# A fused state-space and attention block on one core: front chunks on five PSUM banks, scores of the first stretch from step 6, keys in three transfers

## What is computed

```python
x = x + _L0_conv_ref(_gn(x), ...)      # selective scan block
x = x + _L1_conv_ref(_gn(x), ...)      # attention block

# L0: 96 -> 2*192 channels, depthwise 3x3 conv, four scans of 2304 steps
xz = einsum('bchw,oc->bohw', x, in_proj_w);  xx, z = split(xz, 2)
xx = gelu(depthwise3x3(xx) + conv_b)
xs = stack([x_hw, x_wh, reversed x_hw, reversed x_wh])
dts, Bs, Cs = split(einsum('bkdl,kcd->bkcl', xs, x_proj_w), [R, R + N])
delta = softplus(einsum(dts, dt_w) + dt_b)
h = h * exp(delta * A) + (delta * u) * B;  y = sum_n(h * C)    # 16 states
y = layernorm(sum of the four directions + u * Ds) * gelu(z);  out = out_proj(y)

# L1: 96 -> 3*96 channels, depthwise 3x3 conv, 8 heads of 12
q, k = l2norm(q), l2norm(k)
out = softmax(q @ k.T * SCALE) @ v;  out = w_proj(out)
```

## Time and profile before

| | us |
|---|---|
| median of 3 runs | 11364.33 |
| lowest, highest | 11346.41, 11385.92 |
| the profiled execution's own time | 11346.75 |
| its span in the profile | 11344.6 |
| PE busy | 8357.5 (74%) |
| DVE busy | 7439.6 (66%) |
| ACT busy | 6430.6 (57%) |
| POOL busy | 6332.1 (56%) |

### The profile page before, as it was taken

One profiled execution on the slowest core, in us unless ns is written; L12 is line 12 of the kernel. 1 busy time (PEld: TensorE's weight loads), 2 busy tenths in 40 slices (PEclk: granted clock), 3 DMA queues, 4 the chain that ended last, 5 costly groups with the idle time before them and its releaser, 6 DMA issues.

```text
span 11344.6 us, 176742 instructions
## 1 busy us (share of the span) xinstructions
PE 8357.5 (74%) x54832; PEld 2687.9 (24%) x54832; DVE 7439.6 (66%) x6473; ACT 6430.6 (57%) x11876; POOL 6332.1 (56%) x4464
## 2 busy tenths in 40 slices
PE   6486568887687866888668777678768885588758
PEld 2122222222222222222222222222222221122212
DVE  0588638884488834888358773778548886788630
ACT  1243237773477724776257653667437773577558
POOL 0477527773377724777247662667427774577430
PEclk6565568886798866888678886888768896799779
DMA  1456415653256513555145550555415652455310
GB/s 44 143 181 196 143 49 173 185 175 95 89 183 181 175 52 117 177 178 161 49 150 176 173 166 24 171 184 174 129 54 172 182 178 78 144 184 179 116 23 19
DMA packets 772558, 1537.24 MB, mean 136 GB/s; under 512 B 89368, under 2 KB 416836, under 8 KB 762640
## 3 DMA queue, kind: packets, MB, share of 16 engines
q1 hardware_dynamic: 771600, 1525.54, 44.1%
HBM read 1272.74 MB, written 252.44 MB: 134 GB/s over the span
## 4 chain that ended last, share of the span: by engine, by line
PE 42%; issue 16%; ACT 13%; DVE 12%; DMA 8%; SPq 4%; POOL 4%; ACTq 1%; DVEq 0%; POOLq 0%
PE ps L1549 8%; PE ps L1615 8%; PE ps L1509 6%; ACT probs_buf L1060 4%; PE ps L1537 4%; DVE rings L1281 4%; DVE ps L1260 3%; DMA rep<-xd_scratch 3%; DVE job_buf L1281 2%; ACT rings L1051 2%; PE ps L1703 2%; PE ps L1704 2%; DMA job_u<-u_scratch 2%; PE ps L1566 2%; PE ps L1524 1%
## 5 line engine op out<-in xcount | busy, mean ns | idle before, releaser
L1060 ACT ACTIVATE probs_buf<-ps 128x384 f32<-128x384 f32 x6912 | 3137.8, 491 | 1884.1 <-PE ps L1615 1836.8
L880 POOL TENSOR_TENSOR hc_buf<-rings,rep 128x768 f32<-128x768 f32 x1152 | 2091.6, 1816 | 1711.0 <-DVE rings L1281 1693.8
L1615 PE MATMUL ps<-qp_buf,kp_buf 108*128 108x384 bf16 x6912 | 2299.7, 357 | 623.0 <-ACT probs_buf L1060 274.8
L1260 DVE TENSOR_TENSOR ps<-ps,rep 128x768 f32<-128x768 f32 x2304 | 2182.0, 947 | 826.6 <-PE ps L1525 683.6
L880 POOL TENSOR_TENSOR hc_buf<-job_buf,rep 128x768 f32<-128x768 f32 x1152 | 2092.1, 1816 | 948.7 <-DVE job_buf L1281 941.3
L1537 PE MATMUL ps<-hc_buf,sum_states 128*32 128x144 f32 x24576 | 1530.5, 338 | 135.7 <-POOL hc_buf L880 135.7
L1549 PE MATMUL ps<-probs_buf,v_buf 128*13 128x384 f32 x13824 | 1606.1, 540 | 32.4 <-ACT probs_buf L1060 18.4
L1524 PE MATMUL ps<-st_buf,pick_channel 96*128 96x512 bf16 x2304 | 1009.2, 438 | 652.5 <-DMA qp_buf<-qk_scratch 287.6
L1281 DVE TENSOR_TENSOR_SCAN job_buf<-rings,ps 128x768 f32<-128x768 f32 x768 | 1368.5, 1782 | 167.6 <-ACT rings L1051 142.2
L1615 PEld LDWEIGHTS ps<-qp_buf,kp_buf 108*128 108x128 bf16 x6912 | 652.7, 98 | 3065.6 <-ACT probs_buf L1060 1827.1
L1051 ACT ACTIVATE st_buf<-st_buf,a_cols 128x768 f32<-128x768 f32 x1152 | 1063.2, 927 | 271.4 <-DMA st_buf<-delta_scratch 271.1
(11 more groups left out here) (172 smaller groups left out, 8518.7 us busy)
## 6 DMA issues: line engine op xcount, KB each, us to landing
st_buf<-delta_scratch SPq DMA_DIRECT2D x1152, 384.0 KB
rings<-delta_scratch SPq DMA_DIRECT2D x1152, 384.0 KB
part_scratch<-job_buf SPq DMA_DIRECT2D x1152, 72.0 KB, 3.2
st_buf<-part_scratch SPq DMA_DIRECT2D x192, 432.0 KB, 7.1
rep<-xd_scratch SPq DMA_DIRECT2D x192, 384.0 KB
job_u<-u_scratch SPq DMA_DIRECT2D x192, 192.0 KB
delta_scratch<-job_buf SPq DMA_DIRECT2D x192, 192.0 KB, 4.9
qp_buf<-qk_scratch SPq DMA_DIRECT2D x864, 36.0 KB
```

The costliest lines, as they stand in the source:

```text
L880: pool.tensor_tensor(hc[tile % 2][:, chunk(kk, v)], h_ring[t % 2], rep_third(1, kk, v), ALU.mult).then_inc(s["hc_ready"], 1)
L1060: act.activation(probs[(m % 2) * HG + h], bank(slots["score", p]), ACT.Exp, scale=SCALE)\
L1260: dve.tensor_tensor(u_slot(t), u_slot(t), rep_third(0, kk, t % SPT), ALU.mult)\
L1615: pe.matmul(bank(slots["score", p]), k_parts[:, h, m * 128:(m + 1) * 128], q_ring[:, (kk * NS + q) % 2, h, :], start=True, stop=True).then ...
```

## The change

1. **Front chunks between the scans** (`start` and `back`, not those inside the scan of batch 0). The two projections go to banks 0 and 1, the two convolutions to banks 2 and 3, x_proj to bank 6. The copy of the first convolution is gone: gelu reads both from PSUM. PE issues the projection of chunk c+1 between the convolutions and the x_proj of chunk c, and ACT fills the pads of chunk c+1 right after the gelus of chunk c. SP loads chunk c+1 of the input before it waits for the gelus of chunk c. Since banks 0 to 3 are used, PE waits for chunk 2's pads before the layer norm, and for all copies of q, k, v before the convolutions of chunk 2.
2. **`FRONT_UNITS`, `FRONT_SUMS`**: ACT takes up the gelu part after products 3, 6, 9, 12 and the x_proj copy after products 4, 7, 10, 13; POOL transposes after sums 4, 7, 10, 13.
3. **First stretch of a batch's attention, beside a scan** (`LATE = 6`): no pieces in steps 0 to 5, four to a step in steps 6 to 23. The wait for the queries moves from the head of the stretch to piece 0. The queries of stretch 1 are loaded at steps 12 to 14 instead of 1 to 3.
4. **Keys**: the scratch tensor is laid out by head, so that the three parts of 12 rows stand together; a chunk of keys comes in 3 transfers of 216 KB instead of 9 of 72 KB. The bytes are the same.

The tables and the step's pieces:

```diff
-FRONT_UNITS = ((0, 3, 0, 10), (1, 3, 10, 15), (3, 3, 15, 24),
-               (4, 4, 0, 10), (5, 4, 10, 15), (8, 4, 15, 24),
-               (9, 5, 0, 10), (10, 5, 10, 15), (13, 5, 15, 24),
-               (14, 6, 0, 10), (15, 6, 10, 15))
-FRONT_SUMS = (4, 9, 14)
+FRONT_UNITS = tuple((3 + 3 * (c - 2) + i, c, part) for c in range(2, NPC) for i, part in enumerate(("gelu", "out")))
+FRONT_SUMS = (4, 7, 10, 13)
...
+LATE = 6
...
+def step_scores(t, late=False):
+
+    if late:
+        return range(4 * max(t - LATE, 0), 4 * max(t + 1 - LATE, 0))
+    return range(PER_STEP * t, PER_STEP * (t + 1))
...
-        qk_dram = nc.dram_tensor("qk_scratch", [2, 3, C, L], BF16).ap()
+        qk_dram = nc.dram_tensor("qk_scratch", [2, HEADS, 3, HD, L], BF16).ap()
```

On SP:

```diff
+            def front_chunks(fb):
+
+                front_step(fb, 0, 19)
+                sp.wait_ge(s["f_xn"], (fb + 1) * 16)
+                apart(sp)
+                load_chunk(fb, 0)
+                for c in range(CHUNKS):
+                    if c + 1 < CHUNKS:
+                        load_chunk(fb, c + 1)
+                    front_step(fb, c + 1, 20)
+                    front_step(fb, c + 1, 23)
...
+            def load_keys(hg, c):
+
+                src = qk_dram[1, hg * HG:(hg + 1) * HG, :, :, c * SC:(c + 1) * SC].rearrange("h r d l -> (r d) h l")
+                for t in range(KEY_DMAS):
+                    dst = k_parts[3 * t * HD:3 * (t + 1) * HD, :, c * SC:(c + 1) * SC]
+                    sp.dma_start(dst, src).then_inc(ks_loaded[c], 16)
```

On ACT:

```diff
+            def front_part(fb, c, part):
+
+                n = fb * CHUNKS + c
+                if part == "gelu":
+                    act.wait_ge(s["f_conv"], 2 * n + 2)
...
+                    at_least(act, "f_us", 32 * n)
...
+                    at_least(act, "f_ut", 2 * n)
...
+                    at_least(act, "f_xp", fb * 12 + c)
+                    apart(act)
+                    act.activation(uc[1][:, :], bank(3, 64), ACT.Gelu, bias=conv_bias[1][0:64, :])\
+                        .then_inc(s["f_gelu"], 1)
+                    act.activation(uc[0][:, :], bank(2), ACT.Gelu, bias=conv_bias[0][:, :])\
+                        .then_inc(s["f_gelu"], 1)
+                    act.preload_act_table_set(LN_EXP_TABLES)
+                    if c + 1 < CHUNKS:
+                        front_pads(fb, c + 1)
+                else:
+                    project_out(fb, c)
+                    front_step(fb, c + 2, 2)
```

On PE, `front_in(fb, c)` is the pair of projections of chunk c to banks 0 and 1:

```diff
+            def front_chunk(fb, c):
+
+                n = fb * CHUNKS + c
+                for i, p in ((0, 128), (1, 64)):
+                    pe.wait_ge(s["f_pad"], 2 * n + i + 1)
+                    at_least(pe, "f_gelu", 2 * n)
+                    apart(pe)
+                    for tap in range(9):
+                        ins = pe.matmul(square(bank(2 + i, p)), conv_w[i][:, tap * p:(tap + 1) * p],
+                                        window(pads[i][:, :], tap, 8), start=(tap == 0), stop=(tap == 8))
+                    ins.then_inc(s["f_conv"], 1)
+                if c + 1 < CHUNKS:
+                    front_in(fb, c + 1)
+                pe.wait_ge(s["f_gelu"], 2 * n + 2)
...
+                pe.matmul(bank(BANK_Y), x_proj[0][:, 0:128], uc[0][:, :], start=True, stop=False)
...
                 if fb is not None:
-                    for f in range(3):
-                        front_steps(fb, f)
+                    first_chunks(fb, 2)
+                    pe.wait_ge(s["f_pad"], 2 * (fb * CHUNKS + 3))
                 pe.wait_ge(s["y_summed"], b + 1)
...
                 if fb is not None:
-                    for f in range(3, 7):
-                        front_steps(fb, f)
+                    pe.wait_ge(s["qkv_ev"], (b + 1) * NPC)
+                    for c in range(2, CHUNKS):
+                        front_chunk(fb, c)
```

More of the change, by code:

```diff
@@ L86, in ring_slots @@
     for t in range(BODY):
-        scores = [("score", PER_STEP * t + i) for i in range(PER_STEP)] if att else []
+        scores = [("score", p) for p in step_scores(t, scan and not prev)] if att else []
         order += scores[:2]
@@ L92, in ring_slots @@
             order.append(("proj", 0))
-        if prep and t in JOB_START:
-            order.append(("job", JOB_START.index(t)))
-        order += scores[2:]
+        job = [("job", JOB_START.index(t))] if prep and t in JOB_START else []
+        order += job + scores[2:] if len(scores) < 4 else scores[2:] + job
     ring = (SCAN_RING if att else 1) if scan else RING
@@ L703, in start @@
             def start():
[L704 to L706 removed]
+                front_step(0, 0, 0)
+                front_chunks(0)
                 front_stored(0)
@@ L1053, in stretch @@
                             .then_inc(s["da_ready"], 1)
-                    for p in range(PER_STEP * t, PER_STEP * (t + 1) if att else 0):
+                    for p in step_scores(t, scan and att_first) if att else ():
                         m, h = divmod(p, HG)
@@ L1505, in conv_taps, with first_chunks @@
+            def first_chunks(fb, chunks):
+                front_step(fb, 0, 9)
+                front_step(fb, 0, 13)
+                front_in(fb, 0)
+                for c in range(chunks):
+                    front_chunk(fb, c)
             def conv_taps(fb, i, tap0):
@@ L1630, in sum_part, with next_job @@
                         sum_tile(kidx, q - 1, T + 2 * TG, i)
+                def next_job(j):
+                    free(("job", j))
+                    job(kidx + 1, KS_ORDER[(kk + 1) % K], j, q, slots["job", j])
                 next_m = 0
                 for t in range(BODY):
+                    now = list(step_scores(t, scan and att_first)) if att else []
                     if scan and t == SPG:
```

206 lines of the change are left out of this document (114 added, 92 removed).

## The result

The changed kernel takes **10792.9 us** (median of 4 runs, 10778.2 to 10795.1) against 11355.4 for the kernel before (4 runs beside it): a ratio of 0.9513, 95% interval 0.9486 to 0.9541. I had forecast 11165, at least 11085. The direction was right, but the gain is 562 us where I had 199.

A forecast was written before the change was run, and what follows sets the result against it. The prediction put PE's waits in the front chunks on the path. Start -31, six backs -180, scan heads and first stretches +15, keys -3 sum to -199 us: 11165 us forecast, range 11085 to 11290.

The forecast's parts named there:

- I take the same mixture: Front chunks: the clock keeps mixing its two levels as in the profile, mean 0.76 over two chunks; no gain counted.
- The sign that I had named: Front chunks: the forecast is wrong if the granted clock there leaves 0.6 to 0.8.
- rival 4: Front chunks: clock goes to its full level, a chunk takes 15.5 us; -179 more, 10986 us; chance 0.08.
- Rival 1: Front chunks and backs: clock stays low through denser chunks, +104 us, 11468 us; chance 0.07.
- Start: Six front chunks before the first scan: five idles of 5.9 us and one of 2.4 vanish, -31 us.
- Ahead of the layer norm: Chunks 0 and 1 of six backs: 11.3 us of idle lost, 3.4 of projections added, -8 us each.
- Beside the convolutions: Chunks 2 to 5 of six backs: earlier start and fewer waits, -27 us on PE, -22 us each arriving.
- the tail: ACT and POOL work behind the last gelu, up to the norms: 12.7 us instead of 7.2, giving back 5.5 per back.
- Rival 3: Beside the convolutions: POOL and DVE hold each other up, 12 us net in each of six backs, 11237 us; chance 0.13.
- rival 5: Head of the scan: all of the query wait goes, 40 us and not 4.2, seven times; 10913 us; chance 0.05.
- the -4.2: Head of the scan: moving the query wait gains only 4.2 us each, the rest masked by the u parts.
- Rival 2: First stretch: each step with four pieces takes 4.0 us, +11 in each of seven, 11242 us; chance 0.15.

## Why the prediction was wrong

- **The clock.** The step that failed is "I take the same mixture". It holds the granted clock of the chunks at the level of the rows, and the term for the clock is nothing. Filling the waits and leaving them gave 37 us in start and, in each of six backs, 6.8 ahead of the layer norm, 16.5 in it, 0.8 up to q, k, v and 8.0 beside the convolutions: 37 + 6 x 32.1 = 230 us that the sum had at nothing. The sign that I had named came too: the clock in start's chunks is 1.00, outside 0.6 to 0.8. Against the 568.5 us of the traces my sum of 199 is 369 short: these 230, 74 in the scans and their heads (15 more forecast, 59 less measured, with a scatter of some 20), and the rest in waits and order. The prediction had it as rival 4, with a chance of 0.08. I had set it low by "the layer norm's 0.50 at 94% busy", and that was the wrong reading: PE entered that stage at the low level each time (the x_proj pair ahead of it takes 1.65 us, at the full level 0.91). Entered at the full level, by the changed chunks or by fill, the same stage ran at 1.00.
- **Rival 4's own size**, 10986 us, was short too. Its -56 for start does not follow from its own chunk: six of 15.5 for the 140.9 that the forecast leaves are -48. Its chunk of 15.5 was near (16.8, with a gelu wait of 1.0 that I had at nothing), but it left the layer norm at 38.7 us (6 x 16.5 = 99), and it let DVE and POOL stop the stretch beside the convolutions 6 us below the forecast's.
- **Rival 1**, a clock that stays low in denser chunks, is ruled out. Less idle time raised the clock.
- **Start**: -75, forecast -31. The waits' part, what is left beside the 37 of fill, is at most 38. I also sized a chunk by the first two; the later ones took 30.8.
- **Ahead of the layer norm**: -17.3, forecast -8; the waits' part is at most 10.5.
- **Beside the convolutions**: -37.8, forecast -22. What is left for waits and order, 26.7, is near the -27 that the sum had on PE before the tail took 5.5 back; that they agree is in part chance, since the sum took one back of 129.5 us and the means hold one of 156.4. The tail exists, but now the norms wait 11.78 us for ACT, whose last products wait for POOL's sums, and not for the last gelu. Rival 3 had the wrong sign: the old order was the one in which POOL was blocked, and with its early start no sum took over 5.1 us.
- **Head of the scan**: that the queries' wait was masked by the u parts is right (rival 5 is ruled out); the -4.2 did not come. From the last copy of v to the first broadcast it is 40.7 us before and 40.9 after, means of seven. What took the 4.2 is not shown; a likely cause is SP: in the new layout the stores' issues hold SP 8.9 us, where in the trace of before the same two groups have 1.81 and 3.86, and the rep rows' issues take 8.72, there 6.01.
- **First stretch**: steps 0 to 5 take 18.4 us, I had 16.3, since the first job waits for its u rows; steps 6 to 23 take 55.0 in batch 5 at clock 0.98 (56.7 in the mean), I had 58.5 and 2.5 for a cold start that did not occur. The first stretch grew by 4.2 us, I had +6.3. Rival 2 is ruled out.
- **Keys**: three transfers for nine gain some 3 us at the turn to the second four heads, where I had nothing, at best 5. Nine issues take 10.28 us, 1.14 each and not 0.6. The last attention waits 23.07 us, 5 more and not 3 less, and 24.3 with nine transfers in the new layout: so the number of transfers did not take these 5, and the layout is what is left.

## What to carry to other kernels

Price a wait of PE by what it does to the clock and not only by its length: in these chunks 1.7 us more of idle time cost 6.0, and 16.5 once more in the next stage. To find out, fill the waits with unneeded matmuls before anything is restructured; it is a few lines, and here it was worth some 240 us alone. A stage that is busy at the low level does not show that it must be: read the level of its first matmul and what PE did ahead of it. Where two engines hold each other up, look at where in the other's instruction each one begins, in more than one pass of the loop.

## What the runs showed of the hardware

- A stage of f32 matmuls in which PE is busy 38.04 of 38.8 us stays at 0.50 for all of its 38.7 us when it is entered at the low level, and at 1.00 for 22.2 us when entered at the full one; nothing between was seen in any trace. The rule that I weighed under rival 4 is that of the Trainium skill, "TensorE: Matmul & The Clock Gate", Part 1, where sustained activity releases the clock. The trace agrees with it in the chunks, whose first convolution takes 8.86 us when it is entered low and the next one, of as many matmuls, 5.99, and not in this stage: dense work alone did not release the clock there. Why not is open.
- With one short wait put back in each chunk, the full level was kept into the layer norm in two backs and lost in four of the same execution, in three of them in the 0.57 us of idle ahead of its first matmul: the same instructions do not always end at the same level.
- A POOL sum that comes into DVE's run of convolution steps takes 30.3 us when it comes 0.03 to 0.18 us behind a step's start (3 backs) and 2.6 to 4.2 when it comes 0.9 us or more behind it (15 backs of the old order; 78 of the early one, always at 0.97). What makes the difference is not shown beyond this count, and it holds for the first sum of a back only: later ones came as close to a step's start and took 5.1 us at most. The Trainium skill's page "SBUF — State Buffer" (Who interferes with whom), by which the one that issues first keeps the shared port for the whole instruction, covers a wait for one instruction; a wait over 11 of DVE's steps, as here, does not follow from it.
